# Expert loads one per landed token group, then two parts per tile; eight tiles' rows loaded at once; key copies shared with VectorE

## The reference

```python
# attention: 16 query heads on 4 key heads; the first 896 keys are averaged in blocks of 64,
# the last 128 stay single (142 keys in all)
scores = q_sem @ k_sem2 / sqrt(32) + rope(q_geo) @ pool(rope(k_geo)) / sqrt(32)
scores = where(k_pos <= pos, scores * exp(logit_scale), -1e9)
attn = (softmax(scores) @ v2) @ Wo
# experts: 16, each token takes the best 4 of a softmax router
out = (silu(xn @ gate[e]) * (xn @ up[e])) @ down[e]        # 256 -> 224 -> 256
ffn = sum over the 4 chosen of top_w * out[chosen]
```

## Time and profile before

| what | value |
|---|---|
| median of 3 runs | 399.59 us (397.71 to 400.93) |
| profiled execution, its own time | 400.72 us |
| span in the trace | 398.8 us |
| PE busy | 344.1 us (86%) |
| DVE, ACT, POOL busy | 247.3, 182.6, 221.3 us (62%, 46%, 55%) |
| chain that ended last | PE 61%, DVE 14%, DMA 9%, SPq 6%, issue 5%, ACT 4% |
| mean granted clock of TensorE | 0.957 |

### The profile page before, as it was taken

The page is one execution under the profiler, slowest core; times in us unless marked ns, Lnnn a source line. Parts: engine busy times, 40 slices in busy tenths (PEclk is TensorE's granted clock), DMA queues, the critical chain, the costliest instruction groups (busy, mean ns, idle before and its releaser), DMA issues.

```text
span 398.8 us, 8176 instructions
## 1 busy us (share of the span) xinstructions
PE 344.1 (86%) x2085; PEld 286.4 (72%) x2086; DVE 247.3 (62%) x793; ACT 182.6 (46%) x530; POOL 221.3 (55%) x202
## 2 busy tenths in 40 slices
PE   0499969989899939857786999999999999999991
PEld 0395746446667727656676999999999999999881
DVE  3879984896867836825462885555555555555550
ACT  1541275764024122154373775555555555555450
POOL 1600566566644655886152666666666666666664
PEclk9999998999999988968996999999999999999996
DMA  7992122123282463623796666766666766766544
GB/s 249 365 317 67 54 82 76 71 91 126 86 264 83 148 177 120 220 90 94 234 260 162 99 113 109 109 110 111 110 114 106 108 110 111 114 111 106 70 51 53
DMA packets 50095, 52.35 MB, mean 131 GB/s; under 512 B 5632, under 2 KB 47120, under 8 KB 50072
## 3 DMA queue, kind: packets, MB, share of 16 engines
q0 software_dynamic: 14640, 19.34, 29.2%
q1 hardware_dynamic: 35432, 32.73, 28.2%
HBM read 30.14 MB, written 21.91 MB: 131 GB/s over the span
## 4 chain that ended last, share of the span: by engine, by line
PE 61%; DVE 14%; DMA 9%; SPq 6%; issue 5%; ACT 4%; POOLq 1%; DVEq 0%
PE bank L1380 50%; PE bank L1719 4%; PE bank L1743 4%; DMA wdn<-in_L_ffn_down_proj 3%; DMA xg<-xn_by_expert 2%; DMA x_all<-in_L_attn_x 1%; PE bank L1477 1%; DMA out_rows<-xr 1%; DVE x_keys L1090 1%; DVE lneg L1174 1%; SPq L401 1%; ACT x_all L760 1%; SPq L400 1%; DVE lex L1184 1%; DVE q L1081 1%
## 5 line engine op out<-in xcount | busy, mean ns | idle before, releaser
L738 POOL DMA_INDIRECT out_rows<-y,idx x79 | 123.2, 1560 | 86.0 <-ACT y L932 50.1
L711 POOL DMA_INDIRECT xn_by_expert<-x_all,slot_i x64 | 66.5, 1039 | 53.9 <-DMA xn_by_expert<-x_all,slot_i 31.1
L1358 DVE SCALAR_TENSOR_TENSOR act<-bank,xg,sg 128x224 f32<-128x224 f32 x79 | 35.5, 450 | 49.6 <-ACT sg L919 49.3
L1380 PE MATMUL bank<-wgu_hi,xh 128*128 x158 | 65.8, 416 | 0.0
L1380 PE MATMUL bank<-wgu_lo,xh 128*128 x158 | 59.0, 373 | 0.0
L1380 PE MATMUL bank<-wgu_hi,xl 128*128 x158 | 58.5, 370 | 0.0
L1350 DVE TENSOR_TENSOR xl<-bank,xh 128x256 fp32r<-128x256 f32 x79 | 33.5, 424 | 35.3 <-ACT xh L912 33.6
L919 ACT ACTIVATE sg<-bank 128x224 f32<-128x224 f32 x79 | 28.2, 358 | 56.9 <-PE bank L1380 55.1
L1380 PE MATMUL bank<-wdn_hi,ah 112*128 x158 | 51.6, 327 | 0.8 <-issue 0.7
L1380 PE MATMUL bank<-wdn_hi,al 112*128 x158 | 44.7, 283 | 0.0
L1380 PE MATMUL bank<-wdn_lo,ah 112*128 x158 | 44.5, 282 | 0.0
(11 more groups left out here) (238 smaller groups left out, 650.4 us busy)
## 6 DMA issues: line engine op xcount, KB each, us to landing
xg<-xn_by_expert SPq DMA_DIRECT2D x79, 129.0 KB, 2.5
wgu<-in_L_ffn_gate_proj SPq DMA_DIRECT2D x16, 224.0 KB, 7.0
wgu<-in_L_ffn_up_proj SPq DMA_DIRECT2D x16, 224.0 KB, 7.3
wdn<-in_L_ffn_down_proj SPq DMA_DIRECT2D x16, 224.0 KB, 7.4
x_all<-in_L_attn_x SPq DMA_DIRECT2D x8, 256.0 KB, 4.6
xr<-in_L_attn_x SPq DMA_DIRECT2D x14, 128.0 KB, 8.2
out_rows<-xr SPq DMA_DIRECT2D x14, 128.0 KB
out_rows<-y,idx POOLq DMA_INDIRECT x79
```

The source lines that it names most:

```text
L711: gp.indirect_dma_start(xs_d, bass.IndirectOffsetOnAxis(slot_i[:, z, r:r + 1], 0), x_all[:, z, :], None).then_inc(xs_in[p], DMA)
L738: gp.indirect_dma_start(out_rows, bass.IndirectOffsetOnAxis(idx[r % RING][:, 0:1], 0), ysb[r % 4][:, :], None, compute_op=ALU.add).then_in ...
L1358: nc.vector.scalar_tensor_tensor(av[t.par][:, :], bank[2 + t.par][:, I:2 * I], xg[t.slot][:, D + 1:D + 2], sg[t.par][:, :], ALU.mult, ALU. ...
L1380: return nc.tensor.matmul(o, lhsT, rhs, start=start, stop=stop)
```

## The change

Expert loads. `load_expert` is split in parts. `LATE` has one semaphore for each of experts 4 to 10 and 13, and pairs (11, 12) and (14, 15). In the attention SP loads one expert after each tile's residual: 4 ahead of tile 0's store, then 5 to 8 after tiles 0 to 3, and before each it waits until a number of token groups has landed (`LOADS`). ScalarE splits one expert in each of tiles 2 to 6.

Expert stage. All eight xg buffers are loaded at once, then experts 9 and 10, then the last two sums are stored; after that two parts of experts 11 to 15 follow each of the next eight xg loads. The xg buffers 4 to 7 change places with `al`. ScalarE splits 9 to 15 in steps 2 to 15, VectorE the low parts in steps 3 to 16, POOL only those of 4 to 8. `w_hi` counts parts. The last store has a semaphore of its own (`last_stored`), for which POOL's first scatter and the last high parts wait; the first copy of y waits for the others only.

Key copies. Two of the eight (n = 6, 7) go to VectorE, after `plan_tasks`. On TensorE and ScalarE the queries of batch 1 are turned and copied after key groups 2 and 3, not before. `weights(1)` moves behind the first unit's `diagonals`.

```diff
-LATE = ((4, 5), (6, 7), (8, 9), (10, 11), (12, 13), (14, 15))
+LATE = ((4,), (5,), (6,), (7,), (8,), (9,), (10,), (11, 12), (13,), (14, 15))
...
         wb = r_att[1]
+        xg += [wb.take(f"xg{s}", [P, XW]) for s in range(RING // 2, RING)]
         al = [wb.take(f"al{p}", [IH, 2, P], F32R) for p in range(2)]
-        xg += [wb.take(f"xg{s}", [P, XW]) for s in range(RING // 2, RING)]
...
+        REP_ON_ACT = 6
...
-        SPLITS = ((), (4, 5), (), (6, 7), (), (8, 9), ())
+        SPLITS = ((), (), (4,), (5,), (6,), (7,), (8,))
+        LOADS = ((4, 9), (5, 10), (6, 11), (7, 12), (8, 13))
...
-        IN_LOOP = 10
-        HIGH_FROM, LOW_FROM = 2, 4
+        IN_LOOP = 9
+        HIGH_FROM, LOW_FROM = 2, 3
...
-            def load_late(i):
-                for k in LATE[i]:
-                    load_expert(sp, k, w_late[i])
+            def load_late(k, parts=range(3)):
+                for part in parts:
+                    load_part(sp, k, part, w_late[next(n for n, ks in enumerate(LATE) if k in ks)])
+
+            def load_between(n):
+
+                k, landed = LOADS[n]
+                for p in range(GT):
+                    sp.wait_ge(xs_in[p], landed * DMA)
+                load_late(k)
...
             load_residual(1)
-            load_late(0)
             load_residual(REMOTE - 1)
-
+            load_between(0)
             for i in range(REMOTE - 3):
                 store_sum(i)
                 load_residual(i + 2)
-                if i % 2:
-                    load_late(i // 2 + 1)
+                load_between(i + 1)
             store_sum(REMOTE - 3)
...
-            for j in range(RING // 2):
+            for j in range(RING):
                 load_task(j, j)
-            load_late(3)
+            load_late(9)
+            load_late(10)
             for i in range(REMOTE - 2, REMOTE):
                 store_sum(i)
-            for j in range(RING // 2, RING):
-                load_task(j, j)
-            load_late(4)
-            load_late(5)
...
+            behind = [(k, part) for k in range(11, E) for part in range(3)]
+            for j in range(RING):
+                load_next(j, j, lambda v: v)
+                for k, part in behind[2 * j:2 * j + 2]:
+                    load_late(k, (part,))
-            with sp.Fori(0, LAPS) as i:
+            with sp.Fori(1, LAPS) as i:
...
-                gp.wait_ge(c_stored[u], TB * DMA)
+                gp.wait_ge(c_stored[u], REMOTE * DMA)
+            gp.wait_ge(last_stored, NB * DMA)
...
+            def keep_queries(u):
+                act.wait_ge(l_qt, u + 1)
+                nc.scalar.copy(qrT[u][:, :, :], bank[L_Q[u]][:, :].rearrange("p (g n) -> p g n", g=HKV)).then_inc(l_qT, 1)
             for n in range(2):
                 keep_rep(n)
-            for u in range(NB):
-                act.wait_ge(l_qt, u + 1)
-                nc.scalar.copy(qrT[u][:, :, :], bank[L_Q[u]][:, :].rearrange("p (g n) -> p g n", g=HKV)).then_inc(l_qT, 1)
-            for n in range(2, 2 * HKV):
+            keep_queries(0)
+            for n in range(2, HKV):
+                keep_rep(n)
+            keep_queries(1)
+            for n in range(HKV, REP_ON_ACT):
                 keep_rep(n)
...
                     for u in range(NB):
-                        act.wait_ge(c_stored[u], TB * DMA)
+                        act.wait_ge(c_stored[u], REMOTE * DMA)
...
+                    if n == 2 * (E - IN_LOOP) - 2:
+                        act.wait_ge(last_stored, NB * DMA)
                     split_late(IN_LOOP + n // 2, (n % 2,))
...
-            weights(1)
-
...
             plan_tasks()
+            for n in range(REP_ON_ACT, 2 * HKV):
+                g = n % HKV
+                dve.wait_ge(rep_done, n + 1)
+                for s in range(2):
+                    last = nc.vector.tensor_scalar(rep_g[:, g, :, s, :], bank[REP_BANKS[n]][:, 0:NB * NKEY].rearrange("p (b k) -> p b k", b=NB),
+                                                   sscale[:, s, g:g + 1], None, ALU.mult)
+                last.then_inc(rep_spread, 1)
...
                     build_values()
+                    dve.wait_ge(rep_kept, REP_ON_ACT)
+                    dve.wait_ge(rep_spread, 2 * HKV - REP_ON_ACT)
                     diagonals(bd_g, rep_g, bdg_ready)
+                    weights(1)
...
-                    pe.wait_ge(rep_kept, 2 * HKV)
+                    pe.wait_ge(rep_kept, REP_ON_ACT)
+                    pe.wait_ge(rep_spread, 2 * HKV - REP_ON_ACT)
```

More of the change, by code:

```diff
@@ L336, in build @@
         kv_in, q_in, wo_in, hscale_ready, lscale_ready = sem("kv_in"), sem("q_in"), sem("wo_in"), sem("hscale_ready"), sem("lscale_ready")
-        rep_done, rep_kept, wv_done, vb_built = sem("rep_done"), sem("rep_kept"), sem("wv_done"), sem("vb_built")
+        rep_done, rep_kept, rep_spread, wv_done, vb_built = sem("rep_done"), sem("rep_kept"), sem("rep_spread"), sem("wv_done"), sem("vb_built")
         wrep_ready, masks_ready = sem("wrep_ready"), sem("masks_ready")
@@ L355, in build @@
                                         "p_ready", "p_turned", "pT_ready", "o_done", "out_ready", "out_stored"))
-        c_sum, c_rec = sem("c_sum_ready"), sem("c_rec_ready")
+        c_sum, c_rec, last_stored = sem("c_sum_ready"), sem("c_rec_ready"), sem("last_stored")
         xg_in, scattered = several("xg_in", RING), several("scattered", 4)
@@ L391, in of_expert, with load_part @@
             return w[:, ds(e * width, width)]
-        def load_expert(eng, e, arrived):
+        def load_part(eng, e, part, arrived):
             gate_v = gate.rearrange("e (c p) n -> p e c n", p=P)
@@ L399, in load_expert @@
             dn = of_expert(wdn, e).rearrange("p (c n) -> p c n", c=2)
-            eng.dma_start(gu[:, :, 0:I], gate_v[:, ds(e, 1), :, :].rearrange("p o c n -> p (o c) n")).then_inc(arrived, DMA)
-            eng.dma_start(gu[:, :, I:2 * I], up_v[:, ds(e, 1), :, :].rearrange("p o c n -> p (o c) n")).then_inc(arrived, DMA)
-            eng.dma_start(dn, down_v[:, ds(e, 1), :, :].rearrange("p o c n -> p (o c) n")).then_inc(arrived, DMA)
+            if part == 0:
+                eng.dma_start(gu[:, :, 0:I], gate_v[:, ds(e, 1), :, :].rearrange("p o c n -> p (o c) n")).then_inc(arrived, DMA)
+            elif part == 1:
+                eng.dma_start(gu[:, :, I:2 * I], up_v[:, ds(e, 1), :, :].rearrange("p o c n -> p (o c) n")).then_inc(arrived, DMA)
+            else:
+                eng.dma_start(dn, down_v[:, ds(e, 1), :, :].rearrange("p o c n -> p (o c) n")).then_inc(arrived, DMA)
+        def load_expert(eng, e, arrived):
+            for part in range(3):
+                load_part(eng, e, part, arrived)
         def attended_bank(u, t):
@@ L588, in store_sum @@
                     sp.wait_ge(c_out[u], i + 2)
-                    sp.dma_start(rows(out_rows, u * TB + i), residual(u, i)[:, :]).then_inc(c_stored[u], DMA)
-            def load_late(i):
-                for k in LATE[i]:
-                    load_expert(sp, k, w_late[i])
+                    sp.dma_start(rows(out_rows, u * TB + i), residual(u, i)[:, :]).then_inc(last_stored if i == REMOTE - 1 else c_stored[u], DMA)
+            def load_late(k, parts=range(3)):
[6 more added lines that the diff above has]
+                load_late(k)
             load_residual(0)
@@ L686, in split_low @@
                 if part == 0:
-                    gp.wait_ge(w_hi, e + 1)
+                    gp.wait_ge(w_hi, 2 * e + 2)
                     nc.gpsimd.tensor_tensor(of_expert(wgu_l, e), of_expert(wgu, e), of_expert(wgu_h, e).bitcast(F32), ALU.subtract)
@@ L811, in split_high_part @@
                 if part == 0:
-                    nc.scalar.copy(of_expert(wgu_h, e), of_expert(wgu, e))
+                    nc.scalar.copy(of_expert(wgu_h, e), of_expert(wgu, e)).then_inc(w_hi, 1)
                 else:
@@ L1192, in split_low_part @@
             def split_low_part(e, part):
+                dve.wait_ge(w_hi, 2 * e + part + 1)
                 if part == 0:
-                    dve.wait_ge(w_hi, e + 1)
                     nc.vector.tensor_tensor(of_expert(wgu_l, e), of_expert(wgu, e), of_expert(wgu_h, e).bitcast(F32), ALU.subtract)
@@ L1484, in _, with l_turn_queries @@
                 rep_keys(n)
-            for u in range(NB):
+            def l_turn_queries(u):
                 pe.wait_ge(l_rope, u + 1)
                 turn_queries(bank[L_Q[u]], u).then_inc(l_qt, 1)
+            l_turn_queries(0)
             pe.wait_ge(l_qsT, NB)
@@ L1490, in _ @@
                 rep_keys(n)
+            l_turn_queries(1)
             pe.wait_ge(keys_kept, 1)
```

## The result

| what | before | after |
|---|---|---|
| median in the same session | 398.65 us (397.39 to 400.93, 4 runs) | 384.44 us (381.69 to 388.04, 4 runs) |
| profiled execution, its own time | 400.72 | 381.69 |
| span in the trace | 398.8 | 379.9 |

The ratio is 0.9614, with a 95% interval of 0.9536 to 0.9693. The forecast of 380 in 373 to 389 holds the median, which is 4.4 us above it.

The account below looks back on a forecast made before the run. It took TensorE's chain of waits as the bound, with POOL's token groups next: 400.72 - 14.0 (first row load earlier) - 7.2 (expert stage) + 1.0 (low parts) = 380.5, median 379.4, given as 380, range 373 to 389.

Parts of the forecast that it names:

- Attention: TensorE's two gaps waiting on expert loads (12.7 us) and low clock behind them go, together 15.2; last scores near 166.4.
- rival (c): Attention still waits for loads, SP late behind stores; experts 5 to 8 cost 2.5 us each; 389 us; 6%.
- The gate: What the first row load waits for moves from TensorE (181.6) to POOL's token groups (168): -14.0 us.
- F: Time of the first row load in the expert stage: 183.02 us before, forecast about 169.
- rival (a): Token groups end where they did, 172.9; first row load at 173.9; 385 us; 20%.
- rival (b): Token groups don't feel the loads, TensorE gates at 165.4; first row load 166.5; 378.0 us, or 375; 20%.
- Key copies: Sharing copies between ScalarE and VectorE: net -1.0 us for TensorE up to the attention, worth nothing at the end.
- Expert stage: First row load to tile 9's gate and up shrinks from 36.7 to 29.5 us, both xg gaps gone: -7.2.
- the hold: ScalarE's first copy of y waits 4.1 us for a later store in the expert stage, delaying tile 4.
- Low parts: VectorE's last low part comes a step later, so TensorE stands 1.1 us ahead of tile 18: +1.0.
- The sum: 400.72 - 14.0 - 7.2 + 1.0 = 380.5 for the profiled execution; median 1.1 below, 379.4; given as 380.

Follow-up runs that it names:

- The kernel with the pairs: Changed kernel with attention's part undone: experts 4 to 9 loaded in pairs as before, expert stage still loading eight rows at once; 397.22 us, ratio 0.9915.

## Why the prediction was right, and where it was off

**Attention: right.** Both gaps went, with the low clock behind them, and none came. For the row at 181.64, from which the prediction takes its 166.4 and, with the key copies, 165.4, the changed kernel has 162.08, and 162.98 to 164.87 in the other three profiles. Counted from the first token group, so that a late or early start drops out, this row moved from 140.4 to 123.2 by the mean of four, 17.2 sooner, where 15.2 + 1.0 was said. ScalarE splits at 124.38, 132.69, 140.99, 149.42 and 158.94 with no wait for a load; in the other three profiles it waits at most 1.32 for one, and PE waits for nothing longer than 0.7 between 100 us and the last score. So rival (c) is out. One reading in the prediction is wrong without harm: group 9 is in at 111.36, and 121.55 is the tenth; SP waited 0.4 for group 9 ahead of expert 4.

**The gate: right in place and size, the reason for the size not shown.** It passed to POOL, TensorE idling 5.32 in the first trace and 5.83 to 7.00 in the others (about 5 was said). The groups were to end at 168 from a tenth start at 111.36; by the mean of four profiles it is 111.36 + 57.9 = 169.3. The mean F of the four is (167.24 + 170.61 + 168.56 + 169.87) / 4 = 169.1, for the 169 said. The times of rival (a), F at 173.9, and rival (b), 166.5, are both out for the mean, though single executions range from 167.2 to 170.6. The run times alone would not have told: 384.44 is nearer to the 385 of rival (a) than to 380. The size rested on two readings. One held: a load costs a group 0.9, between the bounds of 0 and 1.43. The other was that three pairs cost 10.2 in the kernel before, from its one trace, and that single loads give much of it back. The kernel with the pairs, at 58.2 by estimate and 59.9 at most from the tenth group, does not bear this out: rival (a)'s reason, that five single loads press about as much as three pairs, stays open, and only its time is excluded. What moved F is that TensorE no longer comes last; that the groups then end near 168 is partly luck.

**Key copies: right.** Worth 1.3 to TensorE and nothing at the end. I gave `weights(1)` for POOL's fifth group "0 (up to +1)". POOL's wait for it is 1.4 in three of the four profiles, and there the fifth group begins 30.15 to 30.30 after the first, as before (30.28), so it costs 0. In the fourth the wait is 3.94 and the group begins 1.1 later. What I left out is that the weights now stand behind maxima that hang on the time of TensorE's matmuls.

**Expert stage: the term that was off, in size.** -7.2 was said for F to tile 9. The four profiles have 31.9, 32.1, 32.1 and 31.2 against 36.7, a mean of -4.9, so 2.3 are missing. The mechanism is as said: no wait for tile 4's or 8's rows, and ScalarE held by the store. The base was right too: without the hold, tile 4 was to be at F + 15.3, and with the stores first it is at F + 15.1 and 15.0. The missing 2.3 go in two parts. Tile 4 comes at F + 18.4 by the mean, not 17.6: the store landed, and ScalarE's first copy of y began, at F + 17.1 instead of 16.5, and tile 4 follows that copy by 1.4, not 1.1. From tile 4 to tile 9 it then takes 13.4 instead of 5 x 2.39 = 11.95: behind the gap the low clock level took 1.5, in the first trace (3.28 - 2.39) + (3.05 - 2.39) = 1.55, for which my sum has nothing, though it counted just that effect behind the gaps of the attention. The gap itself, 3.36 in the first trace and 2.75, 2.19 and 2.24 in the others (2.3 said), is no measure of the hold: it depends also on when TensorE gets to tile 3, which is anywhere from F + 12.4 to F + 13.8.

**Low parts: right.** PE's waits of the changed kernel, 165 to 399:

```profile
PE bank L1755 <- DMA xg<-xn_by_expert: 5.8, 2, 5.3
PE bank L1412 <- DVE xl L1382: 3.4, 1, 3.4
PE bank L1412 <- DVE wdn_lo L1226: 1.0, 1, 1.0
```

**The sum.** F to the end was to be 215.8 - 7.2 + 1.0 = 209.6 and is 212.7, 212.9, 212.9 and 212.0: 3.0 too long by the mean, of which 2.3 is the stage's term; 0.7 is spread over the stage and not resolved. With F as said, 380.5 + 3.0 = 383.5, which is the mean of the four profiled executions and within 2 of the medians (384.44, 385.42, 383.83, 384.12). The other correction, 1.1 from the profiled execution to the median of before, does not show up in the kernel after. The range's lower end, 373, has no sum behind it: rival (b) without the stores' hold is 378.0 - 2.3 = 375.7.

## What to carry to other kernels

When a wait is taken off the critical engine, the gain ends at the next chain, here the token groups; find it in the old trace and cost it from its own quiet and disturbed rows before adding up the gaps, and from more than one trace where the price is a few us. When loads are moved ahead of stores on one queue, ask who waits for the stores' buffers, and let a store that is ready go before the wait that the loads stand behind: here that took 3.7 to 4.8 us off the stretch behind F, and 2.2 off the median by itself. Every gap that a sum leaves on TensorE should be priced with the slow tiles behind it.

## What the runs showed of the hardware that I had not expected

- The low clock level behind the gap of tile 4 cost about the same over a wide range of gaps. Tile 4 to tile 9 takes 11.95 us with the stores first. Behind gaps of 2.10 to 4.76 it takes 13.24 to 13.50 in eight profiles (13.48 behind 3.36, 13.50 behind 2.19, 13.48 behind 4.76). One profile does not fit: with experts 5 to 8 not loaded it takes 14.35 behind a gap of 3.99.
- Nearly the same code can get a different clock early on: 0.85 in one profile and 0.58 in that of the kernel with the stores first, between 58 and 67 us, with PE busy all of the time in both. POOL waited 4.53 instead of 1.38 for the weights. In the profile with the wait of 3.94 the clock was 0.81 there, though, and others with 0.81 to 0.83 waited 1.4 at most, so the clock of that stretch is not the whole cause; that stays open.
- A load's price to a token group is not a fixed one. The tenth group took 10.19 with six transfers of 224 KB beside it in the kernel before and 8.46 with six in the kernel with the pairs, where they had begun 2.3 ahead of the group; with three, issued just as it began, it took 7.54 (a quiet one takes 7.33).
